# The delta stage: another order of VectorE's work in slots 0 to 6, leading tokens added once per four heads, a softplus series of three terms

## Chip, cores and metric

One Trainium2 chip, one of its cores, everything in float32. The metric is the device time of one execution in microseconds (us). Three executions of the kernel before took 3642.28, 3643.24 and 3643.34 us.

## What is computed

The reference is four residual blocks on 2048 tokens of width 512. The change touches the third one only, a gated linear attention with 16 heads of width 128, called the delta stage in the kernel:

```
q = silu(causal_conv4(x @ Wq));  k = silu(causal_conv4(x @ Wk));  v = silu(causal_conv4(x @ Wv))
g = -exp(A_log) * softplus(x @ Wfa @ Wfb + dt_bias)          # decay, per channel
beta = sigmoid(x @ Wb);  q = l2norm(q) * K**-0.5;  k = l2norm(k)
for each token t:                                            # S: 128 x 128 per head
    S = S * exp(g_t);  S += k_t (v_t - S^T k_t) beta_t;  o_t = S^T q_t
out = (rmsnorm(o) * o_norm_w * sigmoid(x @ Wga @ Wgb)) @ Wo
```

Two pieces matter here. The causal convolution has four taps, so the first three tokens of a stretch of tokens need the last three of the stretch before. And softplus(z) = max(z, 0) + ln(1 + w) with w = exp(-|z|); where w is small the logarithm is replaced by its power series in w.

## The kernel before

The program runs an attention stage, a feed-forward stage, the delta stage (`delta_stage`) and a second feed-forward stage. In the delta stage the work is cut into 16 units: four stretches of 512 tokens (TT) by four groups of four heads (HG, HJ). A unit is cut into 16 chunks of 32 tokens, and each chunk is one slot. The stage is a software pipeline over units k: while unit k runs its recurrence, unit w = k + 1 is prepared (convolutions, silu, decays, the small triangular matrices), the first projections of w2 = k + 2 begin, and unit p = k - 1 is finished (normed, gated, multiplied by Wo). Which engine does what in which slot is written out by hand: each engine's block has a loop `for k`, `for sl in range(SLOTS)` with conditions on `sl`, and each engine works through its own queue in exactly that order. A wait at the head of a queue holds all that is behind it.

One slot of the recurrence is this round trip between the engines:

- TensorE, `keys_state` (L1308): state times keys. It waits for the state of the slot before (`s_read`).
- VectorE, `residual` (L997): forms the right-hand side `dl_rbuf` from it.
- TensorE, `solve_u` (L1335): multiplies by the inverse of the triangle. It waits for `residual`.
- ScalarE, `take_u` (L837): copies that to `dl_ubuf`.
- TensorE, `state_step` (L1346): forms the state's increment. It waits for `take_u`.
- VectorE, `add_state` (L1004): new state = decayed state + increment, in `dl_state` and `dl_alt` in turn. It sets `s_read`.

Between these TensorE does work that does not depend on the recurrence: projections (L1366) or output rows (L1373), 128x512 multiplications in two portions per slot, and the short jobs of the table in `short_jobs`. They fill the time of the round trip. ScalarE decays the state (L822), evacuates banks, and applies silu (L861), exp (L945) and sigmoid (L885). Of a projection it first writes tap 0 with the bias (L852) and saves the last three tokens in `dl_tails` (L856).

VectorE's other work, by the names that the diff touches:

- `convolve(u, i, late)`: the taps 1 to 3 of projection i. The early call adds the leading tokens' share (`dl_bnd`, L1017, 3 columns), then taps 1 and 2; the late call does tap 3 and frees the PSUM bank. The twelve projections of a unit are four heads of q, then k, then v.
- `boundary(u)`: the leading tokens' share of all twelve, from the tails of the stretch before.
- `series(u, n)`: the power series of ln(1 + w) by Horner's rule on 2048 columns (L1044, L1047). `near_zero` (L1057) makes the mask, `choose` (L1066) puts the series where the mask is set, `softplus` (L1071) adds max(z, 0).
- `decayed(u, a)` (L1077): q or k times the decay, 2048 columns.
- `o_scale(u, n)` (L1205) and `gated(u, n)` (L1215): norm and gate of the finished unit.

Two waits tie other engines to these. TensorE's use of a PSUM bank for a projection waits until the late tap of the projection two places earlier has read it. And ScalarE's first sigmoid of a unit's gate overwrites `dl_sg`, which the series still reads, so it waits for `series_done`:

```
                        if n == 0:
                            act.wait_ge(s["series_done"], min(u + 3, UNITS))
```

Around the recurrence a slot of VectorE's queue reads: `residual`, early taps, what stands "ahead of `add_state`", `add_state`, late tap, what stands "behind `add_state`", and then the `residual` of the next slot.

Of the kernel before, what the change touches and what calls it, by code (L numbers as in the profile page):

```python
# [624 lines left out]
def delta_stage(nc, x_in, x_out, xnt_dram, ps, cst, d):  # L625

    with ExitStack() as c2:
# [28 lines left out]
        bnd = sb("bnd", [P, 3, HJ, 3])  # L656
# [32 lines left out]
            lambda u: tot2[:, u % 2])  # L689
        by_block = lambda ap: ap[:].rearrange("p g t -> p (g t)").rearrange("p (g t) -> p g t", t=C)  # L690
# [10 lines left out]
            bnd_ready q_silu k_silu v_silu k_square q_square softplus_abs softplus_exp softplus_ln series_done softplus_sum decay_ready  # L701
# [15 lines left out]
        with nc.Block() as block:  # L717
# [87 lines left out]
            def _(act):  # L805
# [178 lines left out]
            def _(dve):  # L984
# [21 lines left out]
                def convolve(u, i, late):  # L1006
# [18 lines left out]
                def boundary(u):  # L1025
# [5 lines left out]
                    o.done(dve.tensor_tensor(bnd[:], tl, taps(0, 3), ALU.mult))  # L1031
                    step(dve.tensor_tensor(bnt[:, :, :, 0:2], tl[:, :, :, 1:3], taps(1, 2), ALU.mult))
                    step(dve.tensor_tensor(bnd[:, :, :, 0:2], bnd[:, :, :, 0:2], bnt[:, :, :, 0:2], ALU.add))
                    step(dve.tensor_tensor(bnt[:, :, :, 0:1], tl[:, :, :, 2:3], taps(2, 1), ALU.mult))
                    dve.tensor_tensor(bnd[:, :, :, 0:1], bnd[:, :, :, 0:1], bnt[:, :, :, 0:1],
                                      ALU.add).then_inc(s["bnd_ready"], 1)

                def series(u, n):
                    w_, poly = flat(sg[:]), kkt(u).rearrange("p g v -> p (g v)")
                    if n == 0:  # L1040
# [187 lines left out]
                for k in range(-2, UNITS + 1):  # L1228
                    w, w2, p = k + 1, k + 2, k - 1
                    run, prep, ahead, post = 0 <= k < UNITS, 0 <= w < UNITS, 0 <= w2 < UNITS, 0 <= p < UNITS  # L1230
                    for sl in range(SLOTS):
# [25 lines left out]
                        if prep:  # L1257
                            if sl == 11:
                                whole_decay(w)
                        if sl == 12 and ahead:  # L1260
                            boundary(w2)
# [9 lines left out]
                        if prep:  # L1271
                            if sl == 0:
                                series(w, 0)
                                series(w, 1)
                            if sl == 1:
                                series(w, 2)
                                near_zero(w)
                            if sl == 2:
                                series(w, 3)
                            if sl == 3:  # L1280
                                softplus(w)
                            if sl == 4:
                                decayed(w, QQ)
                            if sl == 5:
                                decayed(w, KK)
                            if sl == 6:
                                level_take(w, 0)
                            if 6 <= sl <= 10:
                                level_early(w, sl - 5, 0)
                            if sl == 8:  # L1290
                                turn_beta(w)
                            if sl == 11:
                                norm_tables(w)
                                blocks_out(w)
# [303 lines left out]
```

## Time and profile before

| | |
|---|---|
| median of three executions | 3643.24 us |
| the profiled execution, its own time | 3644.98 us |
| its span, first to last instruction | 3642.8 us |
| delta stage within it, about | 920 to 2970 us |
| units 1 to 13 of the recurrence | 1125.4 to 2752.5 us, 13 units of 122.7 to 129.1 us |

The span is what the profile divides into busy time and waits; the profiled execution's own time is 2.2 us more than its span, and 1.74 us more than the median. Units differ by the jobs that only some have: units 3, 7 and 11 also multiply by Wb in slot 4 and by Wga in slot 7, units 2, 6 and 10 by Wfa in slot 9. All other units of the middle have the same jobs.

### The profile page before, as it was taken

What the parts mean: (1) busy time and instruction counts of PE and PEld (TensorE: products, weight loads), DVE (VectorE), ACT (ScalarE), POOL (GpSimd) and SP (SyncE); (2) the same over time, 40 slices, a digit from 0 to 9 for tenths busy, and PEclk for the clock granted to TensorE, in tenths of its full rate; (3) what the DMA queues carried; (4) which work ended last, traced back from release to release, by engine and by line L of the source; (5) the groups of instructions that cost most, each with busy time, mean ns of one, the idle gap of its engine ahead of it and who ended that gap; (6) DMA issues with size and microseconds to landing.
All of it is one profiled execution on the core that took longest, in us unless ns stands there. A gap on an engine that the chain in (4) does not pass through costs nothing. (4 is left out here: it accounts for less than half of the span.)

```text
span 3642.8 us, 85340 instructions
## 1 busy us (share of the span) xinstructions
PE 3432.4 (94%) x37232; PEld 1644.3 (45%) x37232; DVE 1945.9 (53%) x3346; ACT 1429.7 (39%) x3321; POOL 125.0 (3%) x457
## 2 busy tenths in 40 slices
PE   7989999996789999999999999999999869999999
PEld 4444444443344444444445444444544434444444
DVE  2221111113787888789877978888898531111111
ACT  2020000003457656765665576566656531000000
POOL 0000000000000000000000000000000000000000
PEclk9999999998989999999999999999999969999999
DMA  4020100004101111121011211111211033101000
GB/s 165 0 95 0 29 29 0 12 0 152 34 25 34 49 51 38 39 66 41 29 64 38 63 34 46 43 38 40 66 39 36 11 133 95 29 0 29 0 12 12
DMA packets 83725, 156.21 MB, mean 43 GB/s; under 512 B 8782, under 2 KB 33998, under 8 KB 79516
## 3 DMA queue, kind: packets, MB, share of 16 engines
q1 hardware_dynamic: 83356, 150.77, 12.7%
q8 instruction: 295, 4.83, 0.6%
q14 instruction: 74, 0.61, 0.1%
HBM read 133.71 MB, written 17.04 MB: 41 GB/s over the span
## 5 line engine op out<-in xcount | busy, mean ns | idle before, releaser
L1366 PE MATMUL psum<-dl_xt,dl_wqkv 128*128 128x512 f32 x1536 | 777.5, 623 | 11.7 <-DVE dl_qkv L1010 11.7
L541 DVE SCALAR_TENSOR_TENSOR f_act_g<-psum,f_bup,f_act_g 128x512 f32<-128x512 f32 x96 | 72.0, 750 | 930.0 <-ACT f_act_g L495 930.0
L1010 DVE SCALAR_TENSOR_TENSOR dl_qkv<-psum,dl_par,dl_qkv 128x511 f32<-128x511 f32 (+2 forms) x576 | 430.7, 748 | 14.2 <-DVE dl_qkv L1017 0.2
L495 ACT ACTIVATE f_act_g<-psum,f_bgate 128x512 f32<-128x512 f32 x96 | 66.0, 687 | 923.1 <-PE psum L432 923.1
L1366 PEld LDWEIGHTS psum<-dl_xt,dl_wqkv 128*128 128x128 f32 x1536 | 257.5, 189 | 251.2 <-issue 211.8
L432 PE MATMUL psum<-xnt_sb,wup 128*128 128x512 f32 x768 | 345.2, 592 | 0.0
L428 PE MATMUL psum<-xnt_sb,wgate 128*128 128x512 f32 x768 | 345.2, 592 | 0.0
L450 PE MATMUL psum<-f_wdown,f_hidden 128*128 128x512 f32 x768 | 344.9, 592 | 0.0
L1373 PE MATMUL psum<-dl_wo,dl_sg 128*128 128x512 f32 x512 | 261.0, 624 | 3.2 <-DVE dl_qkv L1010 2.8
L428 PEld LDWEIGHTS psum<-xnt_sb,wgate 128*128 128x128 f32 x768 | 145.9, 190 | 183.7 <-issue 183.7
L450 PEld LDWEIGHTS psum<-f_wdown,f_hidden 128*128 128x128 f32 x768 | 145.9, 190 | 183.7 <-issue 183.7
L432 PEld LDWEIGHTS psum<-xnt_sb,wup 128*128 128x128 f32 x768 | 145.9, 190 | 183.7 <-issue 183.7
L852 ACT ACTIVATE dl_qkv<-psum,dl_par 128x512 f32<-128x512 f32 x192 | 148.7, 774 | 200.7 <-PE psum L1366 200.5
L1100 DVE TENSOR_TENSOR dl_kq<-dl_kq,dl_dec 128x512 f32<-128x512 f32 x320 | 206.7, 687 | 4.1 <-PE psum L1416 4.1
L822 ACT ACTIVATE dl_sdec<-dl_alt,dl_tot 128x128 f32<-128x128 f32 x512 | 162.8, 394 | 59.8 <-DVE dl_alt L1004 59.8
L837 ACT ACTIVATE dl_ubuf<-psum 128x128 f32<-128x128 f32 x256 | 70.2, 274 | 272.1 <-PE psum L1335 272.1
L822 ACT ACTIVATE dl_sdec<-dl_state,dl_tot 128x128 f32<-128x128 f32 x512 | 162.8, 395 | 21.8 <-DVE dl_state L1004 21.8
L1335 PE MATMUL psum<-dl_rbuf,dl_zd 32*32 32x128 f32 x2048 | 110.3, 286 | 47.9 <-DVE dl_rbuf L997 46.8
L1346 PE MATMUL psum<-dl_ubuf,dl_kkt 32*128 32x128 f32 x2048 | 132.2, 328 | 23.8 <-ACT dl_ubuf L837 23.8
L1004 DVE TENSOR_TENSOR dl_state<-dl_sdec,psum 128x512 f32<-128x512 f32 x128 | 87.9, 687 | 113.3 <-PE psum L1346 113.3
L1004 DVE TENSOR_TENSOR dl_alt<-dl_sdec,psum 128x512 f32<-128x512 f32 x128 | 87.5, 683 | 113.0 <-PE psum L1346 112.9
L1416 PEld LDWEIGHTS psum<-dl_kq,dl_qkv 128*32 128x32 f32 x10240 | 107.1, 112 | 88.7 <-issue 82.9
(200 smaller groups left out, 4535.0 us busy)
## 6 DMA issues: line engine op xcount, KB each, us to landing
dl_wqkv<-in_dw_qkv SPq DMA_DIRECT2D x192, 256.0 KB, 2.6
dl_wo<-in_dwo SPq DMA_DIRECT2D x16, 1024.0 KB, 5.6
f_weights_b<-f_weights_by_expert SPq DMA_DIRECT2D x48, 256.0 KB, 6.4
wgate<-in_wgate SPq DMA_DIRECT2D x2, 3072.0 KB, 19.4
wup<-in_wup SPq DMA_DIRECT2D x2, 3072.0 KB, 24.6
f_wdown<-in_wdown SPq DMA_DIRECT2D x2, 3072.0 KB, 12.3
x_sb<-in_x SPq DMA_DIRECT2D x4, 1024.0 KB, 9.0
x_after_experts<-x_sb SPq DMA_DIRECT2D x16, 256.0 KB, 2.0
```

The source lines that it names most:

```text
L428: last = pe.matmul(ps[:, 2 * b, :], lhs, xnt[:, k, s * FT:(s + 1) * FT], start=(k == 0), stop=(k == KC - 1))
L432: last = pe.matmul(ps[:, 2 * b + 1, :], wu[:, n, k, c * P:(c + 1) * P], xnt[:, k, s * FT:(s + 1) * FT], start=(k == 0), stop=(k == KC - 1))
L450: last = pe.matmul(ps[:, 4 + i, :], hid[:, b, i * P:(i + 1) * P], rhs, start=(u == 0), stop=False)
L822: last = act.activation(sdec[:, j, :], heads_state(k, sl)[:, j, :], ACT.Copy, scale=tot(k)[:, j, sl:sl + 1])
L852: act.activation(qkv[:, a, j, :], ps[:, bank, :], ACT.Identity, bias=par[:, h, 12 + a:13 + a], scale=par[:, h, 4 * a + 3:4 * a + 4])
L1004: dve.tensor_tensor(heads_state(k, sl + 1), sdec[:, :, :], ps[:, 0:HJ, 0:P], ALU.add).then_inc(s["s_read"], 1)
L1010: tap_ = lambda dl: dve.scalar_tensor_tensor(y_[:, dl:TT], ps[:, bank, 0:TT - dl], par[:, h, 4 * a + 3 - dl:4 * a + 4 - dl], y_[:, dl:TT], ...
L1100: o.done(dve.tensor_tensor(late, late, dv[:, :, :, 0, 0:1].broadcast_to([P, HJ, nb, m]), ALU.mult))
L1335: last = pe.matmul(ps[part(j), UPS, mid], zd(k)[part(j), sl, :], rbuf[part(j), :], start=True, stop=True)
L1346: last = pe.matmul(ps[:, j, 0:P], kkt(k)[part(j), sl, :], ubuf[part(j), sl % 2, :], start=True, stop=True)
L1366: last = pe.matmul(ps[:, bank, :], wq[:, n % RING, m, :], xt[:, u // HG % 2, m, :], start=(m == 0), stop=(m == KC - 1))
L1373: last = pe.matmul(ps[:, bank, :], sg[:, m, P * i:P * i + P], wo[:, m, :], start=(m == 0), stop=(m == HJ - 1))
```

## The change

It does three things in the delta stage.

1. VectorE's order in slots 0 to 6 is new. Series step 0 moves ahead of `add_state` in slot 0, step 2 ahead of it in slot 1; `choose` moves from slot 3 to slot 2, behind `add_state`; `softplus` moves ahead of `add_state` in slot 3; the first two `o_scale` move from slot 2 to slot 3, behind `add_state`; `decayed` of q moves from slot 4 to slot 5, ahead of `add_state`.
2. The leading tokens' share is no longer added once per projection. `edges(u, a)` adds it once for the four heads of q, k or v, behind the late tap of the last of them (slots 0, 4 and 12). ScalarE's silu waits for `edged`, and `dl_bnd` has two copies.
3. The series has three terms instead of four and is used below 2^-8 instead of 2^-6. `series_done` is set by `near_zero` in slot 1; before, it was set by the last series step in slot 2.

The other engines' instructions and their order stay as they are.

```diff
-        bnd = sb("bnd", [P, 3, HJ, 3])
+        bnd2 = sb("bnd", [P, 2, 3, HJ, 3])
...
                 def silu(u, a, signal):
-                    for j in range(HJ):
-                        wait_read(act, "proj", u, 4 * (1, 0, 2)[a] + j)
+                    act.wait_ge(s["edged"], 3 * u + (2, 1, 3)[a])
                     act.activation(qkv[:, a], qkv[:, a], ACT.Silu).then_inc(signal, 1)
...
                     if not late:
-                        if i == 0:
-                            dve.wait_ge(s["bnd_ready"], u + 1)
                         dve.wait_ge(s["tapped"], 12 * u + i + 1)
-                        step(dve.tensor_tensor(y_[:, 0:3], y_[:, 0:3], bnd[:, a, j, :], ALU.add))
                         step(tap_(1))
...
+                def edges(u, a):
+                    dve.wait_ge(s["bnd_ready"], u + 1)
+                    for j in range(HJ):
+                        wait_read(dve, "proj", u, 4 * (1, 0, 2)[a] + j)
+                    dve.tensor_tensor(qkv[:, a, :, 0:3], qkv[:, a, :, 0:3], bnd(u)[:, a], ALU.add).then_inc(s["edged"], 1)
+
...
-                        ins = dve.scalar_tensor_tensor(poly, poly, (1.0 / 3.0, -0.5, 1.0)[n - 1], w_, ALU.add, ALU.mult)
-                        if n == 3:
-                            ins.then_inc(s["series_done"], 1)
-                        else:
-                            o.done(ins)
+                        o.done(dve.scalar_tensor_tensor(poly, poly, (-0.5, 1.0)[n - 1], w_, ALU.add, ALU.mult))
...
-                    o.done(dve.tensor_scalar(flat(kq(u)[:, 1]), flat(sg[:]), 2.0 ** -6, None, ALU.is_lt))
-                    mark[("near", u)] = o.n
+                    o.wait(mark[("series", u, 2)])
+                    dve.tensor_scalar(flat(kq(u)[:, 1]), flat(sg[:]), 2.0 ** -8, None, ALU.is_lt).then_inc(s["series_done"], 1)
...
+                        if prep and sl == 0:
+                            series(w, 0)
+                        if prep and sl == 1:
+                            series(w, 2)
+                        if prep and sl == 3:
+                            softplus(w)
+                        if post and sl == 4:
+                            o_scale(p, 2)
+                            o_scale(p, 3)
                         if post and sl in (5, 6):
                             gated(p, 2 * sl - 9)
-                        if prep and sl == 3:
-                            choose(w)
-                        if post and sl in (2, 4):
-                            o_scale(p, sl - 2)
-                            o_scale(p, sl - 1)
...
+                        if prep and sl == 5:
+                            decayed(w, QQ)
...
+                        if prep and sl in (0, 4, 12):
+                            edges(w, {0: QQ, 4: KK, 12: VV}[sl])
...
+                        if prep and sl == 0:
+                            series(w, 1)
+                        if prep and sl == 1:
+                            near_zero(w)
+                        if prep and sl == 2:
+                            choose(w)
+                        if post and sl == 3:
+                            o_scale(p, 0)
+                            o_scale(p, 1)
+                        if prep and sl == 5:
+                            decayed(w, KK)
```

VectorE's queue from `add_state` of slot 0 to `add_state` of slot 1, before (L1044 and L1047 are series steps, L1192 and L1193 are `o_var`, L1017 the leading tokens, L1010 the taps):

```order
L1004 TENSOR_TENSOR dl_alt<-dl_sdec,psum 128x512
L1010 SCALAR_TENSOR_TENSOR dl_qkv<-psum,dl_par,dl_qkv 128x509
L1044 TENSOR_SCALAR dl_kkt<-dl_sg 128x2048
L1047 SCALAR_TENSOR_TENSOR dl_kkt<-dl_kkt,dl_sg 128x2048
L1192 TENSOR_TENSOR dl_ofac<-dl_oss,dl_kap 128x16
L1193 SCALAR_TENSOR_TENSOR dl_ofac<-dl_ofac,dl_kap 128x16
L997 SCALAR_TENSOR_TENSOR dl_rbuf<-psum,dl_nkap,dl_val 128x128
L1017 TENSOR_TENSOR dl_qkv<-dl_qkv,dl_bnd 128x3
L1010 SCALAR_TENSOR_TENSOR dl_qkv<-psum,dl_par,dl_qkv 128x511
L1010 SCALAR_TENSOR_TENSOR dl_qkv<-psum,dl_par,dl_qkv 128x510
L1004 TENSOR_TENSOR dl_state<-dl_sdec,psum 128x512
```

The same place in the changed kernel, where the lines below L1017 have other numbers (L1047 is step 0, L1050 the other steps, L1026 `edges`, L1191 and L1192 `o_var`):

```order
L1047 TENSOR_SCALAR dl_kkt<-dl_sg 128x2048
L1004 TENSOR_TENSOR dl_alt<-dl_sdec,psum 128x512
L1010 SCALAR_TENSOR_TENSOR dl_qkv<-psum,dl_par,dl_qkv 128x509
L1026 TENSOR_TENSOR dl_qkv<-dl_qkv,dl_bnd 128x4x3
L1050 SCALAR_TENSOR_TENSOR dl_kkt<-dl_kkt,dl_sg 128x2048
L1191 TENSOR_TENSOR dl_ofac<-dl_oss,dl_kap 128x16
L1192 SCALAR_TENSOR_TENSOR dl_ofac<-dl_ofac,dl_kap 128x16
L997 SCALAR_TENSOR_TENSOR dl_rbuf<-psum,dl_nkap,dl_val 128x128
L1010 SCALAR_TENSOR_TENSOR dl_qkv<-psum,dl_par,dl_qkv 128x511
L1010 SCALAR_TENSOR_TENSOR dl_qkv<-psum,dl_par,dl_qkv 128x510
L1050 SCALAR_TENSOR_TENSOR dl_kkt<-dl_kkt,dl_sg 128x2048
L1004 TENSOR_TENSOR dl_state<-dl_sdec,psum 128x512
```

Step 0 went from behind `add_state` to ahead of it, an `edges` came in behind the late tap, and a series step now stands between the early taps of slot 1 and its `add_state`.

VectorE's queue in slots 4 and 5 from the late tap of slot 4 to the `residual` of slot 6, before (L1077 is `decayed`, first of q and then of k, L1215 `gated`):

```order
L1010 SCALAR_TENSOR_TENSOR dl_qkv<-psum,dl_par,dl_qkv 128x509
L1077 TENSOR_TENSOR dl_kq<-dl_qkv,dl_dec 128x2048
L997 SCALAR_TENSOR_TENSOR dl_rbuf<-psum,dl_nkap,dl_val 128x128
L1017 TENSOR_TENSOR dl_qkv<-dl_qkv,dl_bnd 128x3
L1010 SCALAR_TENSOR_TENSOR dl_qkv<-psum,dl_par,dl_qkv 128x511
L1010 SCALAR_TENSOR_TENSOR dl_qkv<-psum,dl_par,dl_qkv 128x510
L1215 SCALAR_TENSOR_TENSOR dl_sg<-psum,dl_onw,dl_sg 128x4x128
L1004 TENSOR_TENSOR dl_state<-dl_sdec,psum 128x512
L1215 SCALAR_TENSOR_TENSOR dl_sg<-psum,dl_onw,dl_sg 128x4x128
L1010 SCALAR_TENSOR_TENSOR dl_qkv<-psum,dl_par,dl_qkv 128x509
L1077 TENSOR_TENSOR dl_kq<-dl_qkv,dl_dec 128x2048
L997 SCALAR_TENSOR_TENSOR dl_rbuf<-psum,dl_nkap,dl_val 128x128
```

The same place in the changed kernel (L1076 is `decayed`, L1214 `gated`, L1026 `edges`):

```order
L1010 SCALAR_TENSOR_TENSOR dl_qkv<-psum,dl_par,dl_qkv 128x509
L1026 TENSOR_TENSOR dl_qkv<-dl_qkv,dl_bnd 128x4x3
L997 SCALAR_TENSOR_TENSOR dl_rbuf<-psum,dl_nkap,dl_val 128x128
L1010 SCALAR_TENSOR_TENSOR dl_qkv<-psum,dl_par,dl_qkv 128x511
L1010 SCALAR_TENSOR_TENSOR dl_qkv<-psum,dl_par,dl_qkv 128x510
L1214 SCALAR_TENSOR_TENSOR dl_sg<-psum,dl_onw,dl_sg 128x4x128
L1076 TENSOR_TENSOR dl_kq<-dl_qkv,dl_dec 128x2048
L1004 TENSOR_TENSOR dl_state<-dl_sdec,psum 128x512
L1214 SCALAR_TENSOR_TENSOR dl_sg<-psum,dl_onw,dl_sg 128x4x128
L1010 SCALAR_TENSOR_TENSOR dl_qkv<-psum,dl_par,dl_qkv 128x509
L1076 TENSOR_TENSOR dl_kq<-dl_qkv,dl_dec 128x2048
L997 SCALAR_TENSOR_TENSOR dl_rbuf<-psum,dl_nkap,dl_val 128x128
```

`decayed` of q left the place ahead of slot 5's `residual` and now stands directly ahead of slot 5's `add_state`.

## Rows read from the trace of the kernel before

**Rows 1.** The page's busy time of each engine, share of span, instructions.

```profile
PE 3432.4 (94%) x37232; PEld 1644.3 (45%) x37232; DVE 1945.9 (53%) x3346; ACT 1429.7 (39%) x3321; POOL 125.0 (3%) x457
```

**Rows 2.** Busy time in two windows: units 1 to 13, unit 0.

```profile
core 0: us, PE busy (x) PEld busy (x) DVE busy (x) ACT busy (x) POOL busy (x), PEclk, DMA share, GB/s
1125.40:2752.50 1627.10, 1575.62 (x27321) 785.00 (x27321) 1350.16 (x2314) 1027.35 (x2496) 97.93 (x364) 1.00 0.15 45
1004.10:1125.40 121.30, 106.23 (x2041) 55.17 (x2041) 96.35 (x164) 75.17 (x185) 7.55 (x28) 0.89 0.11 31
```

**Rows 3.** TensorE's waits in units 1 to 13: total us, times, longest.

```profile
PE psum L1335 <- DVE dl_rbuf L997: 30.0, 36, 1.4
PE psum L1346 <- ACT dl_ubuf L837: 14.0, 26, 0.6
PE psum L1373 <- DVE dl_qkv L1010: 2.6, 10, 0.3
PE psum L1410 <- ACT dl_qkv L861: 2.0, 13, 0.2
```

**Rows 4.** TensorE's timeline, unit 7, slots 1 to 3: start, duration, [idle before].

```profile
1881.17 0.42 PE L1335 MATMUL psum<-dl_rbuf,dl_zd 32*32 32x128 f32 x8 [0.80 <-DVE dl_rbuf L997]
...
1885.77 0.40 PE L1308 MATMUL psum<-dl_state,dl_kq 128*32 128x128 f32 x8
...
1899.01 0.50 PE L1346 MATMUL psum<-dl_ubuf,dl_kkt 32*128 32x128 f32 x8 [0.64 <-ACT dl_ubuf L837]
```

**Rows 5.** VectorE's timeline, unit 7, slots 0 and 1.

```profile
1875.75 0.69 DVE L1004 TENSOR_TENSOR dl_alt<-dl_sdec,psum 128x512 f32<-128x512 f32 x1 [2.11 <-PE psum L1346]
1876.36 0.74 DVE L1010 SCALAR_TENSOR_TENSOR dl_qkv<-psum,dl_par,dl_qkv 128x509 f32<-128x509 f32 x1
1877.01 1.22 DVE L1044 TENSOR_SCALAR dl_kkt<-dl_sg 128x2048 f32<-128x2048 f32 x1
...
1880.77 0.34 DVE L997 SCALAR_TENSOR_TENSOR dl_rbuf<-psum,dl_nkap,dl_val 128x128 f32<-128x128 f32 x1
...
1883.17 0.69 DVE L1004 TENSOR_TENSOR dl_state<-dl_sdec,psum 128x512 f32<-128x512 f32 x1 [0.42 <-PE psum L1346]
```

**Rows 6.** ScalarE's timeline, unit 7, slot 2: the gate's first sigmoid.

```profile
1895.07 0.60 ACT L885 ACTIVATE dl_sg<-psum 128x512 f32<-128x512 f32 x1 [3.56 <-DVE dl_kkt L1047]
```

**Rows 7.** TensorE's timeline, unit 5, slots 4 to 6 and 12.

```profile
1660.72 1.98 PE L1373 MATMUL psum<-dl_wo,dl_sg 128*128 128x512 f32 x4 [0.26 <-DVE dl_qkv L1010]
...
1663.48 0.42 PE L1335 MATMUL psum<-dl_rbuf,dl_zd 32*32 32x128 f32 x8 [0.34 <-DVE dl_rbuf L997]
...
1664.89 0.50 PE L1346 MATMUL psum<-dl_ubuf,dl_kkt 32*128 32x128 f32 x8
...
1666.81 0.43 PE L1308 MATMUL psum<-dl_state,dl_kq 128*32 128x128 f32 x8
...
1716.61 0.42 PE L1335 MATMUL psum<-dl_rbuf,dl_zd 32*32 32x128 f32 x8 [1.28 <-DVE dl_rbuf L997]
```

**Rows 8.** VectorE's timeline, unit 5: slots 5 and 11.

```profile
1663.08 0.34 DVE L997 SCALAR_TENSOR_TENSOR dl_rbuf<-psum,dl_nkap,dl_val 128x128 f32<-128x128 f32 x1
...
1709.18 0.16 DVE L1017 TENSOR_TENSOR dl_qkv<-dl_qkv,dl_bnd 128x3 f32<-128x3 f32 x1
1709.37 1.53 DVE L1010 SCALAR_TENSOR_TENSOR dl_qkv<-psum,dl_par,dl_qkv 128x511 f32<-128x511 f32 x2
1710.82 0.21 DVE L1128 COPY dl_tot<-dl_dec 128x64 f32<-128x64 f32 x1
```

**Rows 9.** ScalarE's timeline, unit 5, slot 4: the tails of projection 8.

```profile
1661.34 0.15 ACT L856 ACTIVATE dl_tails<-psum 128x3 f32<-128x3 f32 x1
```

**Rows 10.** VectorE's groups in units 1 to 13: busy us, mean ns, idle before.

```profile
L1047 DVE SCALAR_TENSOR_TENSOR dl_kkt<-dl_kkt,dl_sg 128x2048 f32<-128x2048 f32 x39 | 89.1, 2284 | 0.4
...
L1066 DVE COPY_PREDICATED dl_kq<-dl_kq,dl_kkt 128x2048 f32<-128x2048 int32 x13 | 33.6, 2587 | 0.0
...
L1017 DVE TENSOR_TENSOR dl_qkv<-dl_qkv,dl_bnd 128x3 f32<-128x3 f32 x156 | 24.3, 156 | 14.7 <-ACT dl_tails L856 14.7
```

More of the change, by code:

```diff
@@ L689, in delta_stage @@
             lambda u: tot2[:, u % 2])
+        bnd = lambda u: bnd2[:, u % 2]
         by_block = lambda ap: ap[:].rearrange("p g t -> p (g t)").rearrange("p (g t) -> p g t", t=C)
@@ L1030, in boundary @@
                         dve.wait_ge(s["tapped"], 12 * (u - HG) + 12)
-                    o.done(dve.tensor_tensor(bnd[:], tl, taps(0, 3), ALU.mult))
+                    o.done(dve.tensor_tensor(bnd(u), tl, taps(0, 3), ALU.mult))
                     step(dve.tensor_tensor(bnt[:, :, :, 0:2], tl[:, :, :, 1:3], taps(1, 2), ALU.mult))
-                    step(dve.tensor_tensor(bnd[:, :, :, 0:2], bnd[:, :, :, 0:2], bnt[:, :, :, 0:2], ALU.add))
+                    step(dve.tensor_tensor(bnd(u)[:, :, :, 0:2], bnd(u)[:, :, :, 0:2], bnt[:, :, :, 0:2], ALU.add))
                     step(dve.tensor_tensor(bnt[:, :, :, 0:1], tl[:, :, :, 2:3], taps(2, 1), ALU.mult))
-                    dve.tensor_tensor(bnd[:, :, :, 0:1], bnd[:, :, :, 0:1], bnt[:, :, :, 0:1],
+                    dve.tensor_tensor(bnd(u)[:, :, :, 0:1], bnd(u)[:, :, :, 0:1], bnt[:, :, :, 0:1],
                                       ALU.add).then_inc(s["bnd_ready"], 1)
@@ L1056, in near_zero @@
                         dve.wait_ge(s["o_ps"], SLOTS * (u - 1))
-                    o.done(dve.tensor_scalar(flat(kq(u)[:, 1]), flat(sg[:]), 2.0 ** -6, None, ALU.is_lt))
-                    mark[("near", u)] = o.n
+                    o.wait(mark[("series", u, 2)])
+                    dve.tensor_scalar(flat(kq(u)[:, 1]), flat(sg[:]), 2.0 ** -8, None, ALU.is_lt).then_inc(s["series_done"], 1)
                 def choose(u):
                     ln, mask = flat(kq(u)[:, 0]), flat(kq(u)[:, 1])
-                    o.wait(mark[("near", u)])
+                    o.wait(mark[("series", u, 2)])
                     dve.wait_ge(s["series_done"], u + 1)
@@ L1249, in _ @@
                             add_rows(*before[1:])
+                        if prep and sl == 0:
[7 more added lines that the diff above has]
+                            o_scale(p, 3)
                         if post and sl in (5, 6):
                             gated(p, 2 * sl - 9)
-                        if prep and sl == 3:
-                            choose(w)
-                        if post and sl in (2, 4):
-                            o_scale(p, sl - 2)
-                            o_scale(p, sl - 1)
[L1257 to L1260, printed above, removed]
+                        if prep and sl == 5:
+                            decayed(w, QQ)
+                        if prep and sl == 11:
+                            whole_decay(w)
+                        if ahead and sl == 12:
                             boundary(w2)
@@ L1268, in _ @@
                             convolve(*conv, True)
+                        if prep and sl in (0, 4, 12):
+                            edges(w, {0: QQ, 4: KK, 12: VV}[sl])
                         if prep and sl == 13:
                             blocks_in(w)
[L1271 to L1294, printed above, removed]
@@ new lines, in _ @@
+                        if prep and sl == 5:
+                            decayed(w, KK)
+                        if prep and sl == 6:
+                            level_take(w, 0)
+                        if prep and 6 <= sl <= 10:
+                            level_early(w, sl - 5, 0)
+                        if prep and sl == 8:
+                            turn_beta(w)
+                        if prep and sl == 11:
+                            norm_tables(w)
+                            blocks_out(w)
@@ L1301, in _ @@
+                        if post and sl == 0:
+                            o_var(p)
+                        if post and sl == 1:
+                            o_factor(p)
             @block.tensor
```

9 lines of the change are left out of this document (2 added, 7 removed).

## Prediction

> **What bounds the kernel now.** I read the page first: TensorE is busy for 94% of the span, VectorE for 53% [rows 1]. The change touches only the delta stage, so the next view is the busy time by windows. In units 1 to 13 TensorE is busy for 1575.62 of 1627.10 us at a granted clock of 1.00, 97%, and VectorE for 1350.16, 83% [rows 2]. So TensorE's own work sets the length of a unit, and an edit on VectorE can give back at most TensorE's idle time: 1627.10 - 1575.62 = 51.5 us in these 13 units. TensorE's waits say who owns it [rows 3]: 30.0 us for `residual` on VectorE, 14.0 us for `take_u` on ScalarE, 2.6 us at L1373 for a late tap that has not freed its bank, 2.0 us at L1410 for the silu of k.
>
> The timelines then give the slots; waits repeat to about a tenth of a us from unit to unit. In every unit: 0.80 us in slot 1 for `residual` and 0.64 us in slot 3 for `take_u` [rows 4], and 1.28 us in slot 12 for `residual` [rows 7]. In the ten units that have no Wb job in slot 4 (all of these but 3, 7 and 11) also 0.26 us at L1373 and 0.34 us in slot 5 for `residual` [rows 7]. These add up to the totals: L1335 is 13 x 0.80, 10 x 0.34 and 13 x 1.25, so slot 12's mean is 1.25. Of L1346, 14.0 - 13 x 0.64 = 5.7 us are left for slot 10; they and the 2.0 us at L1410 hang on chains that the change leaves alone.
>
> **Slot 1: the first 0.80.** Before, the queue behind `add_state` of slot 0 holds the late tap, step 0, step 1 and two small ones; `residual` starts 5.02 us after `add_state`, at 1880.77 [rows 5]. TensorE was ready 0.80 before 1881.17, at 1880.37 [rows 4]. In the changed order step 0 stands ahead of `add_state`, where VectorE idled 2.11 us [rows 5]; its 1.22 fit. Step 0 held the queue for 1.25 (1877.01 to the start of step 1, with its dependence); `edges` comes in. No row shows a 128x4x3 operation. The nearest is the 3-column one, 0.156 us each, and 0.19 from its start to the tap's [rows 8, 10]; the upper end is an operation of 512 columns, 0.69. I take 0.25 with its wait, nearest to the small one. So `residual` starts 1.0 us earlier, at about 1879.8, ends at 1880.15, before TensorE's 1880.37. The whole 0.80 goes; at 0.69 us for `edges`, 0.25 of it stays.
>
> **Slot 1's `add_state` gets later.** Between early taps and `add_state` now stands step 2, 2.28 us each [rows 10]. `residual` at 1879.8, +0.26, +1.45 for two taps (1709.37 to 1710.82 [rows 8]), +2.21 for the step: `add_state` at 1883.7 instead of 1883.17. Behind it is TensorE's `keys_state` of slot 2, before at 1885.77 [rows 4], now wanted at 1884.97. It needs the state about 0.8 us after the start of `add_state` (0.69 and the hand-over): 1884.5. Slack 0.5: no cost.
>
> **Slots 2 and 3: the 0.64.** ScalarE is late with `take_u` in slot 3 because its queue stood 3.56 us at the gate's first sigmoid for the last series step [rows 6]. Now `near_zero` in slot 1 signals, before ScalarE gets there, so that wait goes, and ScalarE reaches `take_u` with about 2 us to spare. `choose`, 2.59 us [rows 10], takes the place of a series step of 2.28 behind slot 2's `add_state` and ends over 1 us before TensorE wants slot 3's `residual`. `softplus` (2048 columns, so again 2.3) ahead of slot 3's `add_state` fits because the early taps no longer wait for ScalarE. The 0.64 goes entirely. All edits so far: 1.44 us per unit.
>
> **Slots 4 to 6, units without the Wb job.** With `decayed` of q gone from slot 4, the late tap frees its bank in time (0.26 goes) and `residual` of slot 5 is about 2 us early (0.34 goes). On unit 5's clock TensorE has gained 0.80 + 0.64 + 0.26 + 0.34 = 2.04 and solves slot 5 at 1661.44. But now VectorE has more to do before slot 5's `add_state`, and its taps wait for the tails of projection 8. They stood behind the exp on ScalarE, ended at 1661.49 [rows 9], and move only with slots 1 and 3, by 1.44, to 1660.05. From there: taps 1.45, `gated` 0.65 (a 512-column step like the late tap's 1876.36 to 1877.01 [rows 5]), `decayed` 2.21: `add_state` at 1664.4. The state step ends at 1665.39 - 2.04 = 1663.35 [rows 7], so `add_state` is 0.9 late, and `keys_state` of slot 6, wanted at 1666.81 - 2.04 = 1664.77 [rows 7], starts at 1665.2: a new wait of 0.44. It covers the old 0.16 at L1410, net 0.28. Behind it the second `gated`, the late tap and `decayed` of k make slot 6's `residual` end 0.15 after TensorE is ready. So these units keep 2.04 - 0.28 - 0.15 = 1.61 after slot 6, ends 1.2 and 2.04. In units 3, 7 and 11 slot 4 is longer by the Wb job, ScalarE and VectorE have caught up by slot 5, and `decayed` hides in the wait for the state step: 1.44.
>
> **Slot 12.** In slots 9 to 12 VectorE runs without a gap up to slot 12's `residual`, which TensorE awaits for 1.28 [rows 7]. Slots 10 and 11 lose one leading-token operation each, 0.19 from its start to the tap's [rows 8]; that comes off the wait: 0.38 per unit.
>
> Here a rule of the Trainium skill speaks against part of it: by "VectorE: DVE Perf Modes", section "The DRAIN you can't avoid", a semaphore between two VectorE operations costs nothing extra. By it only the operation's own 0.156 would go, and the slot 12 term would be 4.1 instead of 4.9 us over 13 units. The rows show 0.19 from start to start, 0.03 over its length.
>
> **Outside units 1 to 13.** Unit 0 has no finished unit beside it and TensorE idles for 15 of its 121.3 us [rows 2]; walked through in the same way it gains 1.5 up to slot 6 and 0.4 in slot 12. Unit 14 gains 1.6 and 0.4. The preparation ahead of unit 0, which VectorE and ScalarE bound, gains about 1.0. Unit 15 nothing.
>
> **Sum.** Slots 1 and 3: 13 x 1.44 = 18.7. Slots 4 to 6: 10 x (1.61 - 1.44) = 1.7. Slot 12: 13 x 0.38 = 4.9. Outside: 1.9 + 2.0 + 1.0 = 4.9. Together 30.2 us. The profiled execution took 3644.98, so 3614.8; it stands 1.74 over the median of the runs, 3643.24, so a median of 3613.0.
>
> **The rivals.**
>
> A. The queue is denser than I walked it, and one of the two big waits stays or comes back: `edges` at 0.69 or more (0.25 per unit), or `keys_state` of slot 2 or 6 later by half a us. Units keep 0.7 to 1.2 instead of 2.0, which is 9 to 17 us in all: 3626 to 3634. For it: the slack is only 0.2 in slot 1 and 0.5 in slot 2. Against: `residual` was early or level in no slot where its queue held less than 3 us.
>
> B. Slower. `add_state` of slot 5 becomes the bound: it now stands behind taps, `gated` and `decayed` of q, which waits for the exp on ScalarE. Each us that the tails or the exp come later than 1660.05 delays `keys_state` of slot 6 by one us in ten units. The gain of these is gone where they come 2.0 us later; the whole is slower once they are over 3 us later, since the other units still gain. At 4 us: 30.2 - 40 = -10, 3653. Against it: nothing is put ahead of the exp on ScalarE, and a 3.56 us wait ahead of it is removed [rows 6].
>
> C. The change moves no time: slot 12 sets the pace of the unit and takes back what slots 1 to 5 give, 3643 less 4.9 for the two operations, 3638. For it: the longest waits are there [rows 3, 7]. Against: a wait that is caused in slots 6 to 11 starts from TensorE's level jobs in slot 6, which come earlier with all the rest.
>
> D. More: unit 0's mean clock is 0.89 [rows 2], which is 0.11 x 121.3 = 13 us of full-clock work lost at most, while TensorE waits for VectorE. If its waits shrink and the clock holds at 2.4 GHz, up to half of that may return, and the slot 5 term may be 2.04: 3605.
>
> By the Trainium skill, "TensorE: Matmul & The Clock Gate", Part 1, the clock is throttled by default and released by activity. It would make D likelier; units 1 to 13 at 1.00 agree with it.
>
> **How the numbers follow.** Forecast 0.62, A 0.19, D 0.08, C 0.06, B 0.05. The predicted time is the forecast's, 3613, whose own range is 3608 to 3620 (slot 5 term between its ends, 10 x 0.4; the outside terms by half). For 8 in 10 it has to reach into A and D: 3605 to 3627. A measurement of this kernel tells about 0.2%, 7.3 us, from no change. Faster by more: forecast, A and D with all, 0.89. Within: C, and a little of B, 0.07. Slower: 0.04.
>
> **What would show it.** TensorE's waits in units 1 to 13 fall from 51.5 to about 26 us: L1335 from 30.0 to about 13, nearly all of it slot 12 at 0.9 each and 0.15 in slot 6; L1346 from 14.0 to about 6; L1373 at nothing; a new one of about 0.4 at L1308 in slot 6, in ten units. The gate's first sigmoid no longer waits for VectorE. VectorE has 10 operations fewer per unit. `edges` near 0.2 us is right, near 0.7 wrong. Unit 5 lasts 120.7 us instead of 122.7. What would make me wrong: a wait of over 1 us at L1308 in slots 2 or 6, or slot 12's wait grown by what slots 1 to 5 gave.

## The result, and the profile after

The changed kernel takes 3611.68 us, the median of four runs (3610.93 to 3613.40), beside 3642.88 for the kernel before, now the median of four as well (3642.28 to 3643.34): a ratio of 0.9915, 95% interval 0.9898 to 0.9932, 31.2 us less. The profiled execution took 3611.68 us, its span is 3609.6.

Busy time in windows of the changed kernel: units 1 to 13, unit 0, unit 14 (the columns are those of [rows 2]):

```profile
1120.20:2721.50 1601.30, 1573.07 (x27321) 784.71 (x27322) 1302.52 (x2185) 1032.20 (x2496) 98.13 (x364) 1.00 0.15 46
1002.20:1120.20 118.00, 104.91 (x2041) 54.65 (x2041) 92.63 (x153) 74.88 (x185) 7.56 (x28) 0.90 0.11 31
...
2721.50:2836.20 114.70, 102.92 (x2052) 54.93 (x2051) 90.36 (x151) 67.21 (x177) 7.47 (x28) 0.94 0.08 23
```

TensorE idles for 1601.30 - 1573.07 = 28.2 us in units 1 to 13, where it idled for 51.5. Its waits there, all of them from 0.5 us up:

```profile
PE psum L1336 <- DVE dl_rbuf L997: 13.8, 13, 1.1
PE psum L1347 <- ACT dl_ubuf L838: 5.7, 13, 0.5
PE psum L1309 <- DVE dl_state L1004: 4.2, 10, 0.4
PE psum L1326 <- issue: 1.5, 1, 1.5
PE psum L1309 <- issue: 1.5, 1, 1.5
PE psum L1411 <- ACT dl_qkv L861: 0.5, 3, 0.2
```

The line numbers are one higher than in [rows 3]. `residual` has 13 waits left, one in each unit, where it had 36. `take_u` has 13 of 26. The late tap of L1373 is gone. One wait is new, `keys_state` for `add_state`, ten times 0.42.

TensorE's timeline in unit 7, slots 1 to 3, where [rows 4] had waits of 0.80 and 0.64 in slots 1 and 3; now no row shows one:

```profile
1863.33 0.42 PE L1336 MATMUL psum<-dl_rbuf,dl_zd 32*32 32x128 f32 x8
...
1871.61 0.42 PE L1336 MATMUL psum<-dl_rbuf,dl_zd 32*32 32x128 f32 x8
...
1880.46 0.50 PE L1347 MATMUL psum<-dl_ubuf,dl_kkt 32*128 32x128 f32 x8
```

VectorE's timeline of the same unit, slots 0 and 1, for [rows 5]. Step 0 has gone ahead of the first `add_state`:

```profile
1858.78 0.69 DVE L1004 TENSOR_TENSOR dl_alt<-dl_sdec,psum 128x512 f32<-128x512 f32 x1 [1.17 <-PE psum L1347]
1859.39 0.74 DVE L1010 SCALAR_TENSOR_TENSOR dl_qkv<-psum,dl_par,dl_qkv 128x509 f32<-128x509 f32 x1
1860.26 0.17 DVE L1026 TENSOR_TENSOR dl_qkv<-dl_qkv,dl_bnd 128x12 f32<-128x12 f32 x1
1860.35 2.29 DVE L1050 SCALAR_TENSOR_TENSOR dl_kkt<-dl_kkt,dl_sg 128x2048 f32<-128x2048 f32 x1
...
1862.85 0.34 DVE L997 SCALAR_TENSOR_TENSOR dl_rbuf<-psum,dl_nkap,dl_val 128x128 f32<-128x128 f32 x1
...
1866.75 0.68 DVE L1004 TENSOR_TENSOR dl_state<-dl_sdec,psum 128x512 f32<-128x512 f32 x1
```

From `add_state` to `residual` it is 4.07 us (1858.78 to 1862.85) instead of 5.02. ScalarE's first sigmoid of the gate, for [rows 6], has no wait in its row:

```profile
1873.68 0.60 ACT L885 ACTIVATE dl_sg<-psum 128x512 f32<-128x512 f32 x1
```

TensorE's timeline in unit 5, slots 6 and 12, for [rows 7]:

```profile
1652.00 0.43 PE L1309 MATMUL psum<-dl_state,dl_kq 128*32 128x128 f32 x8 [0.42 <-DVE dl_state L1004]
...
1701.54 0.42 PE L1336 MATMUL psum<-dl_rbuf,dl_zd 32*32 32x128 f32 x8 [1.06 <-DVE dl_rbuf L997]
```

What stands ahead of that last wait, in unit 5: TensorE's state step of slot 11, and VectorE's timeline from there on. First the changed kernel:

```profile
1695.22 0.50 PE L1347 MATMUL psum<-dl_ubuf,dl_kkt 32*128 32x128 f32 x8
```

```profile
1695.68 0.21 DVE L1127 COPY dl_tot<-dl_dec 128x64 f32<-128x64 f32 x1
1695.87 0.69 DVE L1004 TENSOR_TENSOR dl_state<-dl_sdec,psum 128x512 f32<-128x512 f32 x1
...
1698.34 1.06 DVE L1155 STREAM_TRANSPOSE dl_blocks<-dl_amat 128x512 f32<-128x512 f32 x1
...
1701.14 0.34 DVE L997 SCALAR_TENSOR_TENSOR dl_rbuf<-psum,dl_nkap,dl_val 128x128 f32<-128x128 f32 x1
```

`residual` starts 5.27 us after slot 11's `add_state`. Between them are a late tap, the norm tables and `blocks_out` (L1155 to L1160).

The same state step and `add_state` in the kernel before:

```profile
1710.07 0.50 PE L1346 MATMUL psum<-dl_ubuf,dl_kkt 32*128 32x128 f32 x8
```

```profile
1710.95 0.68 DVE L1004 TENSOR_TENSOR dl_state<-dl_sdec,psum 128x512 f32<-128x512 f32 x1
```

Before, `add_state` starts 0.38 us after the state step's end (1710.57); in the changed kernel it starts 0.15 after it (1695.72).

### The profile page after: what moved, and what is told of

Same layout as the page of the kernel before. It is cut to its first block and busy times, and to the rows that moved or that the text cites. A ratio compares the mean times of both kernels' runs of the same rounds, so it can differ in the third digit from the quotient of the medians.

```text
span 3609.6 us, 85178 instructions
## 1 busy us (share of the span) xinstructions
PE 3428.2 (95%) x37232; PEld 1644.9 (46%) x37232; DVE 1886.7 (52%) x3186; ACT 1434.1 (40%) x3321; POOL 125.2 (3%) x457
## 5 line engine op out<-in xcount | busy, mean ns | idle before, releaser
L1010 DVE SCALAR_TENSOR_TENSOR dl_qkv<-psum,dl_par,dl_qkv 128x511 f32<-128x511 f32 (+2 forms) x576 | 428.6, 744 | 39.0 <-ACT dl_tails L857 32.0
L1347 PE MATMUL psum<-dl_ubuf,dl_kkt 32*128 32x128 f32 x2048 | 132.3, 328 | 17.4 <-ACT dl_ubuf L838 17.4
L997 DVE SCALAR_TENSOR_TENSOR dl_rbuf<-psum,dl_nkap,dl_val 128x128 f32<-128x128 f32 x256 | 87.9, 343 | 101.7 <-PE psum L1309 101.7
```

What stands on the lines that cost most here:

```text
L1010: tap_ = lambda dl: dve.scalar_tensor_tensor(y_[:, dl:TT], ps[:, bank, 0:TT - dl], par[:, h, 4 * a + 3 - dl:4 * a + 4 - dl], y_[:, dl:TT], ...
L1347: last = pe.matmul(ps[:, j, 0:P], kkt(k)[part(j), sl, :], ubuf[part(j), sl % 2, :], start=True, stop=True)
```

## The experiments

The experiments were measured in three groups, each with the kernel before beside it, which took 3644.53, 3643.78 and 3646.31 us. So a difference of a few us between kernels of different groups means little, and each experiment is read twice, by its median and by TensorE's waits in units 1 to 13 of its trace. These repeat: the changed kernel, traced a second time, has the same rows to 0.2 us, but for two single ones marked "issue". The first two are the kernel before with one part of the change; all others start from the changed kernel.

**Step 0 alone.** The series' first operation moves ahead of slot 0's `add_state`.

```
+                        if prep and sl == 0:
+                            series(w, 0)
                         if sl == 12 and ahead:
                             boundary(w2)
                         ...
                             if sl == 0:
-                                series(w, 0)
                                 series(w, 1)
```

> The kernel before with one edit: the series' first operation stands ahead of slot 0's add_state, where VectorE idled 2.11 us. Theory (a wait of TensorE is priced by the slot that it stands in): residual of slot 1 starts about 1.2 us earlier and TensorE's 0.80 us in slot 1 go in every unit; the 0.64 us for take_u in slot 3 stay, since ScalarE still stands at the gate's sigmoid for the last step of the series, and slots 5 and 12 stay as they are. 13 x 0.80 plus about 1.3 in units 0 and 14: 11.7 us, about 3631. Rival (slot 12 sets the pace of the unit): it takes the 0.80 back, 3643. Rival (waits in slots 1 and 3 are one chain): both go, 22 us, 3621.

3631.54 us, beside 3644.53 for the kernel before (ratio 0.9967, 0.9954 to 0.9980). Its waits:

```profile
PE psum L1336 <- DVE dl_rbuf L997: 19.7, 23, 1.4
PE psum L1347 <- ACT dl_ubuf L837: 13.8, 26, 0.6
PE psum L1374 <- DVE dl_qkv L1010: 2.6, 10, 0.3
```

`residual` loses 13 waits and 10.3 us, 0.79 a unit; the other rows are those of [rows 3] to 0.2 us. Slot 12 takes nothing back. The 3631 expected came.

**The series alone.** Three terms below 2^-8 in place of four below 2^-6, and `near_zero` signals ScalarE; VectorE's order stays.

```
-  o.done(dve.tensor_scalar(poly, w_, -0.25, None, ALU.mult))
+  o.done(dve.tensor_scalar(poly, w_, 1.0 / 3.0, None, ALU.mult))
...
-                            if sl == 2:
-                                series(w, 3)
```

> The kernel before with the three-term series alone (used where sigmoid is below 2^-8), its signal to ScalarE given by near_zero; the order of VectorE's work is the old one but for the step that is gone. Theory: the signal for the gate's sigmoid comes about 2 us earlier, so the 0.64 us of slot 3 go; the 0.80 us of slot 1 stay; the waits of 0.26 and 0.34 in slots 4 and 5 stay in the main, since decayed of q then waits for the exp on ScalarE. 13 x 0.64 plus about 1 outside: 9 to 11 us, about 3633. Rival (less VectorE work pays in full): one step of 2.28 us less in 15 units is 34 us, 3609.

3632.00 us (ratio 0.9964, 0.9950 to 0.9978). Its waits:

```profile
PE psum L1329 <- DVE dl_rbuf L997: 33.5, 36, 1.4
PE psum L1340 <- ACT dl_ubuf L837: 5.8, 13, 0.5
```

`take_u` loses its 13 waits of slot 3, 14.0 - 5.8 = 8.2 us. The late tap's waits (2.6) are gone, but `residual` has 3.5 more, in slot 5 (0.67 in unit 5, before 0.34): slots 4 and 5 keep their 0.6 us together, as expected, in one place instead of two. That is 8.2 + 2.6 - 3.5 = 7.3 us net for 13 x 2.28 = 30 us of VectorE's time.

**The fourth term back, behind slot 1's `add_state`.**

```
                         if prep and sl == 1:
+                            series(w, 3)
                             near_zero(w)
```

> The changed kernel with the fourth term of the series (used below 2^-6) put back, behind slot 1's add_state, everything else in the new order. Theory: residual of slot 2 comes 2.2 us later against a slack of about 2.04 us, a wait of 0.2 us per unit; near_zero ends at about 1871.4 on unit 7's clock and ScalarE reaches the gate's sigmoid at 1873.7, so no wait there. +3 us, about 3615. Rival (less VectorE work pays in full): +2.2 x 15 = +33, 3645. Rival (all of it lies in idle time of VectorE): 0, 3612.

3622.59 us (3618.43 to 3627.43; ratio 0.9941, 0.9926 to 0.9956). The trace is of the fastest of the four executions, 3616.1 of span. TensorE's and VectorE's timelines, unit 7, slot 2:

```profile
1875.10 0.42 PE L1337 MATMUL psum<-dl_rbuf,dl_zd 32*32 32x128 f32 x8 [0.34 <-DVE dl_rbuf L997]
```

```profile
1871.08 2.28 DVE L1050 SCALAR_TENSOR_TENSOR dl_kkt<-dl_kkt,dl_sg 128x2048 f32<-128x2048 f32 x1
1873.47 1.23 DVE L1057 TENSOR_SCALAR dl_kq<-dl_sg 128x2048 f32<-128x2048 f32 x1
```

The wait is 0.34 in twelve of the 13 units and 0.69 in unit 5, not 0.2: line L1337 has 18.7 us in 26 waits, 4.9 us over the changed kernel. `near_zero` waits for the step just ahead of it, and starts 2.39 us after it, not 2.2; 2.39 less the slack of 2.04 that the expectation had is the 0.35. The waits thus account for 5 us. The median stands 11 over the changed kernel's of another group; the rest isn't explained.

**The fourth term back, ahead of slot 2's `add_state`.** The same arithmetic, another place.

```
+                        if prep and sl == 2:
+                            series(w, 3)
                         if prep and sl == 3:
                             softplus(w)
```

> The changed kernel with the fourth term of the series back (used below 2^-6, as in the kernel before), its step this time ahead of slot 2's add_state, where VectorE idles 2.65 us, and it signals ScalarE. Theory (a VectorE operation costs what of it sticks out of the idle time at its place): 2.28 fit into 2.65, and the step ends at about 1873.2 on unit 7's clock, before ScalarE's sigmoid at 1873.7: no wait appears, 3612. Rival (less VectorE work pays wherever it stands): +2.28 x 15 = +34, 3646. Rival (the sigmoid comes late): up to 0.5 us per unit in slot 3's take_u, +7, 3619.

3613.93 us (3612.06 to 3616.16), beside 3611.87 for the changed kernel in the same group (below); the intervals are 0.9900 to 0.9929 and 0.9895 to 0.9928. VectorE's timeline in unit 7, slot 2, and the waits:

```profile
1871.56 2.28 DVE L1050 SCALAR_TENSOR_TENSOR dl_kkt<-dl_kkt,dl_sg 128x2048 f32<-128x2048 f32 x1
...
1874.29 0.69 DVE L1004 TENSOR_TENSOR dl_alt<-dl_sdec,psum 128x512 f32<-128x512 f32 x1 [0.45 <-PE psum L1353]
```

```profile
PE psum L1342 <- DVE dl_rbuf L997: 13.8, 13, 1.1
PE psum L1353 <- ACT dl_ubuf L838: 5.9, 13, 0.5
PE psum L1315 <- DVE dl_state L1004: 4.3, 10, 0.4
```

These are the changed kernel's waits to 0.2 us, and VectorE still idles for 0.45 us behind the step. So the fourth term costs TensorE nothing there, and the medians differ by less than their intervals. What the change gained by the series it gained by where the last step stands and so when the signal comes, not by less arithmetic.

**Leading tokens once per head again.**

```
-                    act.wait_ge(s["edged"], 3 * u + (2, 1, 3)[a])
+                    for j in range(HJ):
+                        wait_read(act, "proj", u, 4 * (1, 0, 2)[a] + j)
...
+     step(dve.tensor_tensor(y_[:, 0:3], y_[:, 0:3], bnd(u)[:, a, j, :], ALU.add))
...
-                        if prep and sl in (0, 4, 12):
-                            edges(w, {0: QQ, 4: KK, 12: VV}[sl])
```

> The changed kernel with the leading tokens added once per head and projection again, twelve small operations per unit in place of three. Theory: slots 10 and 11 have one operation each, 0.19 us from its start to the tap's, in a queue that is partly late: 0.19 us per unit come back in slot 12 (1.06 to 1.25), and 0.19 us in slot 6 of ten units (0.42 to 0.61), where the taps of slot 5 lead to its add_state. Slots 0 to 3 gain 0.08 from the missing edges and lose nothing. +4 to +5 us, about 3616. Rival (VectorE has idle time enough): 0, 3612. Rival (each operation counts): 9 x 0.19 x 15 = 26 us, 3637.

3620.14 us (3616.89 to 3624.60; ratio 0.9934, 0.9920 to 0.9949). Its waits, and VectorE's timeline ahead of slot 11's `add_state`:

```profile
PE psum L1338 <- DVE dl_rbuf L998: 16.3, 13, 1.4
PE psum L1311 <- DVE dl_state L1005: 6.2, 10, 0.6
```

```profile
1698.44 0.21 DVE L1131 COPY dl_tot<-dl_dec 128x64 f32<-128x64 f32 x1
1698.56 0.69 DVE L1005 TENSOR_TENSOR dl_state<-dl_sdec,psum 128x512 f32<-128x512 f32 x1
```

Both waits are 0.19 to 0.20 larger, as expected: 16.3 / 13 = 1.25 and 0.62. The window of the 13 units is 5.0 us longer (1606.30), also as expected; the median is 8.5 over the changed kernel's of another group, and what is beyond 5 isn't explained.

Two operations are back in slots 10 and 11 and only one shows in slot 12. Slot 11's `add_state` tells why. It starts 0.12 after the copy ahead of it, on its heels. In the changed kernel it starts 0.19 after (1695.68 to 1695.87), since it now waits for TensorE's state step. Unit 5 shows little of it. In the eleven units other than 4 and 8 the three traces read, in us:

| kernel | `add_state` of slot 11 starts after the state step's end | wait in slot 12 |
|---|---|---|
| before | 0.28 to 0.44 | 1.21 to 1.37 |
| changed | 0.13 to 0.15 | 1.06 or 1.07 |
| leading tokens per head | 0.29 to 0.48 | 1.21 to 1.39 |

In units 4 and 8 the three kernels are alike, with 0.13 to 0.15 and 1.06 or 1.07: there the state step came last already before the change, and nothing was to be gained.

**`decayed` of q back in slot 4.**

```
-                        if prep and sl == 5:
-                            decayed(w, QQ)
...
+                        if prep and sl == 4:
+                            decayed(w, QQ)
```

> The changed kernel with decayed of q put back from ahead of slot 5's add_state to behind slot 4's. Theory: residual of slot 5 is late again, since decayed of q waits for the exp on ScalarE, about 0.7 us in ten units; the 0.42 us for keys_state in slot 6 go. Net +0.3 in ten units, +3.2 us, 3615. Rival (the wait for keys_state in slot 6 is a pure cost of the new place): -4 us, 3608.

3614.50 us (3611.59 to 3620.06). Unit 5, slot 5, and the waits:

```profile
1651.87 0.42 PE L1336 MATMUL psum<-dl_rbuf,dl_zd 32*32 32x128 f32 x8 [0.67 <-DVE dl_rbuf L997]
```

```profile
PE psum L1336 <- DVE dl_rbuf L997: 20.6, 23, 1.1
...
PE psum L1411 <- ACT dl_qkv L861: 2.0, 13, 0.2
```

Ten waits of 0.67 for `residual` come, and the ten of 0.42 at `keys_state` go. With 1.5 more at L1411 and 0.9 less in slot 6's solve that is 3.1 us more, as expected. The wait at `keys_state` was the smaller of two prices.

**The finished unit's gate first in slot 5, the norms later, and both.** The first edit, "gate first", puts one `gated` into the 0.77 us that VectorE waits for the tails in slot 5; the second, "norms later", takes ScalarE's inverse norms out of the way of slot 10's `take_u`.

```
+                        if post and sl == 5:       # gate first
+                            gated(p, 1)
                         if conv:
                             convolve(*conv, False)
...
+                        if sl == 10 and prep:      # norms later
+                            inverse_norms(w)
...
-                        if sl == 9 and prep:
-                            inverse_norms(w)
```

> The changed kernel with slot 5's gated of the finished unit ahead of the early taps instead of behind them, in the 0.8 us in which VectorE waits there for the tails. Theory: slot 5's add_state comes 0.65 us earlier, keys_state of slot 6 waits 0.1 instead of 0.42 us and the solve behind it is level: 0.35 to 0.44 us in ten units, -4 us, 3608. Rival (slot 12 takes it back, its residual hangs on a VectorE queue without slack): 0, 3612.

> The changed kernel with ScalarE's inverse norms moved from slot 9 to slot 10, behind take_u. Theory: TensorE's wait of 0.46 us for take_u in slot 10 goes; the wait of 1.06 us in slot 12 grows by nearly as much, since VectorE has 5.27 us of queue between slot 11's add_state and slot 12's residual and its norm tables wait for the inverse norms. Net -1 us, 3611. Rival (waits are separate): -0.46 x 13 = -6 us, 3606. Rival (the tables come late): slot 12 grows by over 1 us, +8, 3620.

> The changed kernel with both: gated ahead of the early taps in slot 5, and the inverse norms in slot 10 behind take_u. Theory: the sum of the two alone, -4 and -1: 3607. Rival (slot 12 gives all back): 3612.

Gate first took 3608.81 us (3605.25 to 3610.45), norms later 3612.00 (3610.65 to 3617.91), both 3607.22 (3604.66 to 3609.38), each within a us of what was expected. The medians alone don't tell them from the changed kernel, since the intervals of the ratios overlap; the waits do. Those of gate first, then of norms later:

```profile
PE psum L1338 <- DVE dl_rbuf L997: 13.8, 13, 1.1
...
PE psum L1413 <- ACT dl_qkv L861: 2.0, 13, 0.2
```

```profile
PE psum L1336 <- DVE dl_rbuf L997: 17.7, 13, 1.6
PE psum L1309 <- DVE dl_state L1004: 4.3, 10, 0.4
```

Gate first removes slot 6's two waits and adds 1.5 at L1411: 4.2 + 0.9 - 1.5 = 3.6. Norms later removes 5.7 in slot 10 and pays 3.9 in slot 12, from 13.8 to 17.7: a wait ahead of a VectorE queue that is already late is mostly given back at the queue's end. With both, slot 12 pays as much (17.4).

**Slot 12's queue cut.** The last four operations of `blocks_out` go behind slot 12's `residual`.

```
                         if run:
                             residual(k, sl)
+                        if prep and sl == 12:
+                            blocks_rest(w)     # L1157 to L1160
```

> The changed kernel with residual of slot 12 drawn ahead of the last four operations (1.7 us) of the 5.27 us of VectorE's queue that stands between slot 11's add_state and it; no work is added or removed. Theory (this queue alone makes TensorE's 1.06 us in slot 12): residual ends at about 1699.8 on unit 5's clock where TensorE wants it at 1700.48, so the 1.06 go in every unit. add_state of slot 12 stays where it is, and keys_state of slot 13 has 0.4 us to spare. 13 x 1.06 plus about 2 in units 0 and 14: 16 us, 3596. Rival (VectorE's chain from slot 6 on is the bound as a whole): the wait moves to keys_state of slot 13, 0 to -3, 3610. Rival (GpSimd's solve starts 0.3 later and blocks_in with it): +4, 3616.

**The three edits together**, and the changed kernel again beside them:

> The changed kernel with three edits: gated ahead of the early taps in slot 5, the inverse norms in slot 10 behind take_u, and slot 12's residual ahead of the last four operations of its queue. Theory: with slot 12 no longer bound, what the first two give is kept: 0.35 us in slot 6 of ten units, 0.44 in slot 10, 1.06 in slot 12 of thirteen: 3.5 + 5.7 + 13.8 = 23, and about 3 outside: 26 us, 3586. The margin for keys_state in slot 13 is 0.1 us. Rival (slot 13's keys_state wait takes over): 0.3 us or more per unit stay, 3592. Rival (VectorE's whole chain binds): no better than the two edits without the third, 3607.

> The changed kernel itself, beside the three that follow, so that they can be compared on one chip. 3612 us by every theory; how far its median and its interval lie from the first measurement says what a difference between kernels of two calls can tell.

| kernel | median us | ratio to before |
|---|---|---|
| before | 3646.31 | |
| changed | 3611.87 (3611.51 to 3615.09) | 0.9911 (0.9895 to 0.9928) |
| queue cut | 3597.66 (3593.19 to 3600.02) | 0.9868 (0.9854 to 0.9883) |
| all three | 3587.65 (3584.87 to 3588.40) | 0.9841 (0.9826 to 0.9856) |

The waits of the kernel with the queue cut, then of that with all three edits:

```profile
PE psum L1351 <- ACT dl_ubuf L838: 5.8, 13, 0.5
PE psum L1313 <- DVE dl_state L1004: 4.2, 10, 0.4
```

```profile
PE psum L1315 <- issue: 2.3, 1, 2.3
PE psum L1417 <- ACT dl_qkv L861: 2.0, 13, 0.2
PE psum L1332 <- issue: 1.8, 1, 1.8
```

Slot 12's 13.8 us are gone whole, with no operation fewer, and no wait has come up in slot 13. With slot 12 free, the 5.7 us of norms later are kept. Both medians are within 2 us of the 3596 and 3586 expected. The window of units 1 to 13 is 1579.80 us and TensorE busy for 99.6% of it:

```profile
1119.00:2698.80 1579.80, 1573.64 (x27321) 785.16 (x27322) 1301.10 (x2184) 1032.22 (x2496) 98.99 (x364) 1.00 0.15 47
```

This is the fastest kernel of the study. In it VectorE waits for GpSimd's solve at slot 13's `blocks_in`, 5.3 us in 13 waits, where the changed kernel's trace lists none. No wait of TensorE comes of it yet. In unit 5:

```profile
1704.04 0.35 DVE L1167 TENSOR_SCALAR dl_blocks<-dl_half,dl_dconst 128x256 f32<-128x256 f32 x1 [0.55 <-POOL dl_half L798]
```

## Why the prediction was right

The forecast was 3613.0, the measurement 3611.68, and the mechanism held: the waits that it named went, and the new one came where it said. That the total is within 1.3 us is in part luck. Slot 12 gave 2.5 less than its term and the time outside units 1 to 13 gave 2.5 more; another 2.5 us came from no term; and the 1.74 us taken off for the profiled execution didn't recur, since that of the changed kernel is at its median.

- **Slots 1 and 3, 18.7 us: right.** Step 0 alone takes 10.3 out of `residual`'s waits and the series alone 8.2 out of `take_u`'s: 18.5, where the 13 x 1.44 stood.
- **`edges`, 0.25: 0.31.** It is 0.171 us long, but from the late tap to step 1 it takes 0.96 us (1859.39 to 1860.35), 0.65 before. `residual` came 0.95 us earlier (1.0 forecast) and slot 1's `add_state` 7.97 us after slot 0's (7.42 before), 0.55 later where 0.5 stood. Neither slack was used up, so rival A's waits never came.
- **Slots 4 to 6, 1.7 us: 2.4.** `keys_state` waits 0.42 (0.44 forecast). The waits of 2.6, 3.4 and 2.0 us made way for 4.2, 0.5 and about 0.9, ten times 0.09 at slot 6's solve, where I had 0.15.
- **Slot 12, 4.9 us: 2.4.** This step failed: "Slots 10 and 11 lose one leading-token operation each; that comes off the wait: 0.38 per unit". The wait went from 1.25 to 1.06, 0.19. I took VectorE's run as gapless up to slot 12, and 1.28 for every unit. The run was gapless in eleven units; in units 4 and 8 `add_state` of slot 11 already waited for TensorE's state step and the wait was 1.06. With 0.38 less in front it meets the state step in all units, and only the queue behind it remains, 5.27 us. So there were at most 0.14 to 0.30 us to gain, in eleven units. Both tests agree: with the two operations back 1.25 returned, and with 1.7 us of that queue moved all 1.06 went.
- **Outside, 4.9 us: 7.4.** It is 33.2 of span less 25.8 in units 1 to 13: preparation 1.9 (1.0 forecast), unit 0 3.3 (1.9), unit 14 2.4 (2.0), and 0.2 the other way behind it. TensorE's idle time fell by 2.0 us in unit 0 and by 2.3 in unit 14, so the waits there were about right. The rest of unit 0 is TensorE's busy time, 106.23 to 104.91 us for the same instructions. The excess of 0.9 in the preparation can't be laid to the change: the start of the first `add_state` lies between 1000.6 and 1004.3 in the 14 traces, at 1002.20 in the changed kernel and at 1003.97 in that with gate first, whose preparation is the same.
- **A surplus of 2.5 us** in units 1 to 13 is TensorE's busy time, 1575.62 to 1573.07, with the same 27321 instructions. The experiments show 1571.20 to 1575.66, so a gain of this size in busy time says nothing of an edit. What makes it is open.

Of the rivals, A did not come, and its argument against reads the wrong way round: in the rows before, `residual` was late in slots 1, 5 and 12 alone, with 5.02, 4.42 (unit 5) and 5.27 us from the `add_state` ahead of it. B did not come either: the wait at slot 6 was 0.42, not the us or more of late tails. C is refuted by step 0 alone (slot 12 gave back nothing) and yet half right: the edit "norms later" shows that slot 12 does take back what is given in slot 10. The argument against C, that slot 12's chain starts at the level jobs of slot 6, was tested only by waits ahead of slot 6, and holds for them. D's clock moved a little: unit 0 went from 0.89 to 0.90 and lost 1.3 us of busy time, of the 13 that D named as the most. (D's two terms at full size would give 3602, not 3605.)

On the price of a hand-over within VectorE the Trainium skill, "VectorE: DVE Perf Modes", section "The DRAIN you can't avoid", has it that a semaphore costs nothing extra; it measured copies. With the fourth term back, the operation that waits for the step just ahead of it started 2.39 us after that step; the independent `add_state` started 2.20 us after one of the same length (1864.55 to 1866.75). This pair disagrees by 0.19 us, if the following operation's kind doesn't matter. Of the two estimates for slot 12, 4.1 and 4.9 us, the measured 2.4 bears out neither.

## What to carry to other kernels

Price an edit at the slot's own wait: the same step of 2.28 us a unit, 30 us of VectorE's time over 13 units, cost nothing in one place, 5 us in another and 7 in a third, where a signal hung on it (all by TensorE's waits). Ahead of the operation that the bound engine waits for, look for work that it doesn't need, and put that behind it: drawing slot 12's `residual` past four operations gave 14 us with nothing removed. When a queue gets shorter, ask where it next meets the other engine; the saving is cut there, and a wait ahead of such a queue is worth removing only once the queue is cut.

## What was not expected of the hardware

TensorE's busy time in unit 14 followed the granted clock, between kernels that hardly differ in that unit. The changed kernel's is at the top. The window of unit 14 in the kernel with the series alone:

```profile
2739.70:2858.40 118.70, 107.15 (x2052) 58.02 (x2052) 92.77 (x157) 67.51 (x177) 7.48 (x28) 0.90 0.07 22
```

It is 4.0 us longer than the changed kernel's unit 14, with 4.2 us more TensorE busy time for the same instructions at a mean of 0.90 instead of 0.94. The other traces agree: unit 14 has 102.8 to 104.0 us of busy time in the five with a mean clock of 0.93 or 0.94, and 105.4 to 107.4 in the nine with 0.90 or 0.91. The kernel before and the changed kernel are both in the first group, so the 2.4 us between them in unit 14 stand. A difference between the groups is as large as most single edits here, so such a unit can't tell two kernels apart; TensorE's waits in the units at a clock of 1.00 can. What puts a trace into one group or the other is not shown.
